# One order string for every iteration of a two-layer attention kernel, in place of eight that repeat

## The chip, the cores and the metric

The kernel runs on one core of one Trainium2 chip. The metric is the device time of the program in microseconds (us). Before the change three runs took 1636.75, 1638.75 and 1639.05 us; the median is 1638.75 us.

## The reference, cut to what matters

The input `x` is 4 x 1024 x 256, the context `ctx_1024` is 4 x 154 x 256. A transformer block (self attention with 16 heads, cross attention to the context, a gated feed-forward) is followed by a second, single-head attention to the same context:

```
x = attention(ln32(x, ln1_s, ln1_b), ln32(x, ln1_s, ln1_b), Wq1, Wkv1, Wo1, bo1) + x
x = attention(ln32(x, ln2_s, ln2_b), context, Wq2, Wkv2, Wo2, bo2) + x
x = geglu_ff(ln32(x, ln3_s, ln3_b), Wff1, bff1, Wff2, bff2) + x
...
attn = softmax((x @ Wq.T + bq) @ (ctx @ Wk.T + bk).T)
x = attn @ (ctx @ Wv.T + bv) + x
```

Self attention over 1024 keys is the largest part. Its softmax subtracts the row maximum, so the scores are computed twice: once to find the maximum, once for the exponential.

## The kernel before, in words

The 4096 rows of `x` are cut into 16 chunks of 256 rows (`NCH`), four to a batch element. A chunk passes through five stages. In `pre` it is normalised and projected to q, k and v, which go to DRAM. In the attention stage it has four units of four heads. `mid` is the output projection, the residual, the second normalisation and q of the cross attention. `cross` is the cross attention. `last` is its output projection, the feed-forward and the second layer.

The stages of different chunks run beside each other. Iteration n (4 to 21) has `pre` of chunk n, attention mostly of chunk n-5 (a little earlier for its maxima), `mid` of chunk n-6, `cross` of chunk n-7 and `last` of chunk n-8. The chunks 0 to 3 have their `pre` in a head before the loop. Iteration 21 (`END`) has what is left: `mid` of chunk 15, `cross` of 14 and 15, `last` of 13, 14 and 15.

What sets the order of work is a string of letters for each iteration. Every engine (SyncE, called SP, issues nearly all DMAs) walks the same string with the function `walk`. At each letter it does its own share of that step, if it has one, and it takes its instructions strictly in that order. Engines are tied to each other by semaphores alone, so SP or ScalarE may be far ahead of TensorE in the string until a wait holds it. The letters are:

- `M`: one 128x512 tile of scores for the maximum (TensorE, line 1679, into one of two PSUM banks) and its reduction (VectorE, line 1360). The matmul of one M waits for the reduction of the M before the last.
- `S`: two score matmuls (line 1697, one of two banks) and one exponential (ScalarE, line 1143). `V`: 16 passes of probabilities times values (line 1709). `Q`, `T`: the maximum of a unit is finished, transposed and stored as two extra rows of q. `O`, `o`: the unit's output is copied (line 1149) and stored (line 801). `u`: q and k of a later unit are loaded.
- `p`, `m`, `c`, `l`: the next step of the chains `pre` (8 steps), `mid` (9), `cross` (36) and `last` (26). In iteration 21 `g` is `cross` of chunk 15, and `k` and `j` are `last` of chunks 14 and 15.
- `x`: q (four DMAs) for `cross` of the next chunk is loaded; for the first chunk of a batch element k and v as well (nine DMAs, lines 714 to 732). `d`: the softmax sums of a cross-attention chunk are loaded (line 672). `i`: VectorE inverts them (line 1244) and SP stores the inverses (line 676). `e`, `f`: the outputs and the inverses are loaded for `last`.
- `s`: a step of the preparation of weights and context.

Steps of `last`, counted from 0, that the text below names: 2 multiplies outputs and inverses (VectorE, line 1249), 3 is the output projection (TensorE, line 1494), 4 the residual and the statistics (VectorE, lines 1255 and 1221), 5 the normalisation, 6 the transposition, 7 to 14 the first feed-forward product (line 1622) with the gate on ScalarE and VectorE, 15 to 18 the second product (line 1631), 19 to 25 the second layer. Step 1 of `mid` inverts the sums of self attention. Steps 1 to 12 of `cross` are its maxima, 13 finishes them, 16 to 35 are scores and values.

There are eight strings: one each for iterations 4 to 7, `STEADY` for 8 to 15, `LATE` for 16 to 19, `FINAL` for 20 and `ENDING` for 21.

Of the kernel before, what the change touches and what calls it, by code (L numbers as in the profile page):

```python
# [21 lines left out]
NCH = B * S // CH  # L22
# [5 lines left out]
NU = NCH * HG  # L28
# [32 lines left out]

FIRST = (
    "sspsssssppsMsMpMMsMsMMpMssMMMMMsMMMpQTMMsMMMMpMpMMsMMsMMs"
)

SECOND = (
    "MMSpSMSQSTSSMMSVSMSMVSMSMSMSMSspSMSVSMMpSsMMSSVMOSpMSSMQVSSTVSMM"
    "sMSSMpMMSSuVSMoSMpSMMVSMoMOpMSMSMSMQusTSSVSMSMSMSMVSMoSMspMMSsMM"  # L70
    "sSSMMVOSMSMVMMQsSSTsSMMSVMSMSMSSMMVMMSSMSMSMSMSMVuMSsMSQVTuO"
)

THIRD = (
    "SSsMMSSMoSMVMSMSSMMVMSMSMuSMSMSMSMSMVpQSmTSVpMOSSMMpSVMSMmSpMSMV"
    "MsSSMpMMSSMpMMSSmVSMuMQpToSVmMOpSoMSMSMSMSMSMSmSsMVMSSVsmMMSSMSo"
    "MSMmSMSMVSQsTmMMVMsOSMSMSMSMVMSMSMSMSSmMMSSMVMusMQxSS"
)

FOURTH = (  # L80
    "sVTSSMMVMsSMSMSOcMuSMScMcuSSMcVMScMSVcSMcSMSopMcSMSSMcSQcVSTScVS"
    "pMSMccOSMSpVSMSMcScpScMSVMSMmpMMcmSMSMcpMcMVMSmSoMcpuQcSTVcmcMSM"
    "pcSMSMcMSMcSMmSOMcSMVcmSMSoMcVSMSMcSMmMcSMQSVuTScSMScMSOVcSMMScm"
    "MMcMdSSMVmMSMSMVMSMSMSeSMixMSSQoVfTVO"
)

STEADY = (
    "uoMSMlcSmpMSMMSSMMSlMMSMcSSMMcVlMMSScclcMuMSScVQSSlccTSSlVScSMcS"
    "MlSmOScMVcMSplMSSpVScMSlpVcMMSlcSMScMpMSlMcSoSVMlMScSpcMMQlTmcpc"
    "MMSclcSVSMpMcSOSMlcMMuSSVVcSSMcMSlocumMMocmSlMmSSMlMlMcMlVQcmTSc"  # L90
    "OVMSmMMclmMSSMcMlSMSMcSMSMVlSMSdMlSMSMVMMQxiSSleTSSVfVlO"
)

LATE = (
    "lMScMMSMSMSuMSlMMSMccSMSMVlcMScMSlMcMSMSQlVcoScSTSVScSlMMSScclSM"
    "VcMcSlOMccSMSSclSmMSVMlSMcMmVScSSMMlcMSSMclMVMSmQcuSlSTcSScVmcSu"
    "oOmMSMclSmSMVcVMSlSmMMclSMcMSmSScMoMlMScMlMMlcSlMMVcmQTlcMVuMSMS"
    "cMlcMOSMScMxSMSVlSMSMMSSMlSMSMdVeMMSSQlSTVViofOl"
)

FINAL = (
    "MMlScSMSMMlSSMMSMMMScMScMVSlMSccMuSlcSMSMcSQVoSlcTclSmVSMMSccSlM"
    "SVccmSMSlMcSSOcMlSVSMMlcMcSSVMSScMMlcMMScSlSVSMcMQSlmcVcSScOmcSm"
    "SVSmSclSScTSmlSSVocoSmclmclclSllSVcSlcSSVcOSclScSlSxVSSSlSSdeVSi"
    "SlSlfOVVo"
)

ENDING = (
    "ccccccccclccocccmcllclcccccccmcmlmclcmlcmccclmlmlkclclcmlcgclxlc"
    "dllllilgggklgeglggggglggkfgglgkkgggglggjggggklkgjggggkggggkgkkkd"  # L110
    "ikkekjkjkkfjkjkjkjjjjjjjjkjjjjjkkjjkkjjjj"
)


def order_of(n):

    if n < LAST_LAG:
        return (FIRST, SECOND, THIRD, FOURTH)[n - MAX_LAG]
    return STEADY if n < NCH else LATE if n < END - 1 else FINAL if n < END else ENDING


CT_STEPS = 3
# [19 lines left out]
def last_set(o):  # L142

    return int(o == NCH - 2)
# [17 lines left out]
def xattn_kernel(nc, t, out):  # L162

    ctx = ExitStack()
    with ctx:
# [340 lines left out]
        def _(sp):  # L506
# [171 lines left out]
            def load_sums(dst, rows, done):  # L678
                for k in range(KD):
                    sp.dma_start(dst[:, k, :], rows.rearrange("(k h w) s -> k h w s", k=KD, w=W)[k, :, 0:DH, :]  # L680
                                 ).then_inc(done, 16)
# [146 lines left out]
        def _(pool):  # L828
# [98 lines left out]
            def last(o):  # L927
                e = last_set(o)
                if e == 0:
                    pool.wait_ge(c_outst, min(o, NCH - 2) * 16)  # L930
                add_bias(xbs[e], x1[1 - (o + LAST_LAG) % 2], bo2, c_xb[1])
                for _ in range(4):
                    yield
                rstd(mv[1], ve[1], rs[1], c_mv[1], c_ve[1], c_rs[1], o + 1)
                yield
                pool.wait_ge(c_x[1], o + 1)
                add_bias(xbs[e], x2s[e], bff2, c_xb[2])
                for _ in range(LAST_STEPS - 5):
                    yield
# [816 lines left out]
```

## Time and profile before

| | |
|---|---|
| median of three runs | 1638.75 us |
| span of the profiled execution, first to last instruction | 1641.9 us |
| TensorE busy (matmul) | 1557.9 us, 95%, 12833 instructions |
| VectorE busy | 1103.1 us, 67% |
| ScalarE busy | 995.2 us, 61% |
| GpSimd busy | 252.9 us, 15% |
| DMA | 129.76 MB, 79 GB/s |
| mean granted TensorE clock | 0.983 |

The profile is of one execution. Its time outside the profiler isn't shown by itself; what is known of it is its span, 3.15 us over the median of the runs. Matmuls are pipelined and the profile models their ends, so TensorE can be "busy" without a pause and still be slower than it could: what counts is the time from the start of one matmul to the start of the next.

### The profile page before, as it was taken

What the parts mean: (1) busy time and instruction counts of PE and PEld (TensorE: products, weight loads), DVE (VectorE), ACT (ScalarE), POOL (GpSimd) and SP (SyncE); (2) the same over time, 40 slices, a digit from 0 to 9 for tenths busy, and PEclk for the clock granted to TensorE, in tenths of its full rate; (3) what the DMA queues carried; (4) which work ended last, traced back from release to release, by engine and by line L of the source; (5) the groups of instructions that cost most, each with busy time, mean ns of one, the idle gap of its engine ahead of it and who ended that gap; (6) DMA issues with size and microseconds to landing.
All of it is one profiled execution on the core that took longest, in us unless ns stands there. A gap on an engine that the chain in (4) does not pass through costs nothing.

```text
span 1641.9 us, 33969 instructions
## 1 busy us (share of the span) xinstructions
PE 1557.9 (95%) x12833; PEld 1011.8 (62%) x12833; DVE 1103.1 (67%) x2269; ACT 995.2 (61%) x2024; POOL 252.9 (15%) x342
## 2 busy tenths in 40 slices
PE   6899999999999999999999999999999999998887
PEld 5454545675757666675767667565656656574766
DVE  4667776858676776858677686858677675843433
ACT  4365667666667566666657566666656555664342
POOL 1210412111112021111112021010011010101110
PEclk9999999999999999999999999999999989997999
DMA  9914242555231412645131321356121311303210
GB/s 236 206 39 139 69 71 83 103 108 109 63 84 46 82 51 72 113 98 119 58 86 47 70 58 58 80 98 116 44 73 35 71 42 44 82 31 73 56 34 13
DMA packets 177116, 129.76 MB, mean 79 GB/s; under 512 B 40975, under 2 KB 168889, under 8 KB 176697
## 3 DMA queue, kind: packets, MB, share of 16 engines
q1 hardware_dynamic: 176889, 127.58, 33.0%
q8 instruction: 101, 1.65, 0.4%
q14 instruction: 62, 0.51, 0.1%
q10 hardware_dynamic: 64, 0.02, 0.0%
HBM read 79.24 MB, written 47.71 MB: 77 GB/s over the span
## 4 chain that ended last, share of the span: by engine, by line
PE 71%; DVE 14%; DMA 7%; ACT 3%; SPq 2%; issue 2%; POOL 0%; DVEq 0%; ACTq 0%; POOLq 0%
PE ps_o L1709 11%; PE ps_max L1679 10%; PE ps_last L1622 10%; PE ps_s L1697 9%; PE ps_last L1631 6%; DVE mxh L1360 6%; PE ps_pre L1486 4%; PE ps_cross L1590 4%; DVE mx L1286 3%; PE ps_pre L1494 3%; PE ps_cross L1576 3%; DMA o_s<-den_c 2%; DMA den<-o_s 2%; PE ps_last L1644 1%; PE ps_last L1659 1%
## 5 line engine op out<-in xcount | busy, mean ns | idle before, releaser
L1360 DVE TENSOR_REDUCE mxh<-ps_max 128x1 f32<-128x512 f32 x1024 | 655.8, 683 | 175.2 <-PE ps_max L1679 173.3
L1143 ACT ACTIVATE probs<-ps_s 128x512 f32<-128x512 f32 x1024 | 579.4, 597 | 232.2 <-PE ps_s L1697 185.4
L1679 PE MATMUL ps_max<-kst,qst 96*128 96x512 bf16 x1024 | 371.5, 386 | 22.0 <-DVE mxh L1360 14.7
L1697 PE MATMUL ps_s<-qst,kst 98*128 98x256 bf16 x2048 | 368.2, 275 | 6.1 <-ACT probs L1143 4.3
L1697 PEld LDWEIGHTS ps_s<-qst,kst 98*128 98x128 bf16 x2048 | 178.8, 98 | 146.6 <-ACT probs L1143 49.4
L1709 PE MATMUL ps_o<-probs,vg 128*17 128x256 f32 x4096 | 268.4, 384 | 0.0
L1679 PEld LDWEIGHTS ps_max<-kst,qst 96*128 96x128 bf16 x1024 | 96.0, 97 | 146.5 <-DVE mxh L1360 91.2
L1087 ACT ACTIVATE probs<-ps_cross 77x512 f32<-77x512 f32 x224 | 132.7, 592 | 78.1 <-PE ps_cross L1576 77.2
L1318 DVE SCALAR_TENSOR_TENSOR th<-th,gb 128x256 f32<-128x256 f32 x128 | 56.9, 445 | 164.3 <-ACT gb L1118 164.3
L1709 PEld LDWEIGHTS ps_o<-probs,vg 128*17 128x17 f32 x4096 | 96.5, 97 | 110.4 <-issue 49.8
L1622 PE MATMUL ps_last<-y_hi,wff_hi 128*128 128x256 f32 x448 | 139.6, 312 | 4.8 <-DVE y_lo L1312 2.5
L1622 PE MATMUL ps_last<-y_lo,wff_hi 128*128 128x256 f32 x448 | 126.9, 283 | 0.0
L1622 PE MATMUL ps_last<-y_hi,wff_lo 128*128 128x256 f32 x448 | 126.6, 283 | 0.0
L1631 PE MATMUL ps_last<-wff,hT 128*128 128x256 f32 x480 | 113.1, 380 | 1.9 <-DVE hT L1321 1.9
L1116 ACT ACTIVATE th<-ps_last,b_tanh 128x256 f32<-128x256 f32 x112 | 53.0, 473 | 89.7 <-PE ps_last L1622 89.7
L1631 PEld LDWEIGHTS ps_last<-wff,hT 128*128 128x128 f32 x480 | 88.9, 190 | 17.2 <-DVE hT L1321 4.3
L885 POOL TENSOR_TENSOR qk_f<-qk_f,qk_parts 128x512 f32<-128x512 f32 x40 | 46.4, 1160 | 323.1 <-ACT qk_f L1076 172.7
L1622 PEld LDWEIGHTS ps_last<-y_hi,wff_hi 128*128 128x128 f32 x448 | 85.3, 190 | 16.0 <-DVE hT L1321 8.4
L1576 PE MATMUL ps_cross<-q2st,k2st 98*77 98x256 bf16 x448 | 86.3, 274 | 2.5 <-ACT probs L1087 2.5
L1622 PEld LDWEIGHTS ps_last<-y_lo,wff_hi 128*128 128x128 f32 x448 | 85.7, 191 | 0.6
L1622 PEld LDWEIGHTS ps_last<-y_hi,wff_lo 128*128 128x128 f32 x448 | 85.6, 191 | 0.0
L876 POOL TENSOR_SCALAR ve<-mv 128x2 f32<-128x2 f32 x34 | 7.7, 226 | 442.7 <-DVE mv L1224 442.7
(261 smaller groups left out, 1951.7 us busy)
## 6 DMA issues: line engine op xcount, KB each, us to landing
parts_s<-qk_parts SPq DMA_DIRECT2D x28, 384.0 KB, 4.3
o_s<-o_sb SPq DMA_DIRECT2D x64, 128.0 KB, 2.6
o_s<-o_sb SPq DMA_DIRECT2D x32, 256.0 KB, 2.2
oT<-o_s SPq DMA_DIRECT2D x62, 128.0 KB
den<-o_s SPq DMA_DIRECT2D x62, 128.0 KB
q_s<-qk_parts SPq DMA_DIRECT2D x16, 384.0 KB, 2.3
q2st<-q_s SPq DMA_DIRECT2D x16, 384.0 KB, 5.3
q2st<-q_s SPq DMA_DIRECT2D x48, 128.0 KB, 6.1
```

The source lines that it names most:

```text
L1087: nc.scalar.activation(probs2[:, h % PR2, :], cross_banks[spare][h % 2][0:CT, :], ACT.Exp, scale=SCALE).then_inc(c_e, 1)
L1143: nc.scalar.activation(probs[:, step % PR, 2 * pair:2 * pair + 2, :].rearrange("p j q -> p (j q)"), ps_s[pair][:, :], ACT.Exp, scale=SCALE ...
L1318: nc.vector.scalar_tensor_tensor(th[:, m % 2, :], th[:, m % 2, :], 1.0, gb[:, m % 2, :], ALU.add, ALU.mult).then_inc(c_gt, 1)
L1360: nc.vector.tensor_reduce(mxh[:, i % PAIRS, i // PAIRS:i // PAIRS + 1], ps_max[i % 2][:, :], AX_X, ALU.max).then_inc(g_mx, 1)
L1486: last = mm(bank[:, m * CH:(m + 1) * CH], w[:, k, m * P:(m + 1) * P], y[:, k, :], start=(k == 0), stop=(k == KD - 1))
L1576: last = mm(cross_banks[spare][h % 2][0:CT, a * CH:(a + 1) * CH], k2st[:, at, a * CT:(a + 1) * CT], q2st[:, at, :], start=True, stop=True)
L1590: last = mm(ps_cross[j * W:j * W + VW, 0:CH], v2[:, a, i * VW:(i + 1) * VW], probs2[:, i % PR2, a * CH:(a + 1) * CH], start=(a == 0), stop ...
L1622: last = mm(last_banks(o)[m % 2][:, part * CH:(part + 1) * CH], wff1[w][:, k, cols_], y3[y][:, k, :], start=(i == 0), stop=(i == len(terms ...
L1631: last = mm(bank_[:, i * D:(i + 1) * D], hTs[e][:, m, i * P:(i + 1) * P], wff2[:, m, :], start=(m == 0), stop=(m == FM - 1))
L1679: mm(ps_max[i % 2][:, :], qst[0:ROWS, h, q * P:(q + 1) * P], kst[0:ROWS, h, half * 512:(half + 1) * 512], start=True, stop=True).then_inc( ...
L1697: last = mm(ps_s[pair][:, j * CH:(j + 1) * CH], kst[:, h, kt * P:(kt + 1) * P], qst[:, h, :], start=True, stop=True)
L1709: last = mm(ps_o[j * W:j * W + VW, 0:CH], vg[:, g, kt, j * VW:(j + 1) * VW], probs[:, step % PR, j, :], start=(kt == 0), stop=(kt == KT - ...
```

## The change

The tuple `ORDERS` holds 18 strings, one for each iteration, and `order_of` picks by iteration. Each letter occurs as often in all 18 as before (3969 letters), and the chains still begin and end in the same iterations, but the shared letters (S, M, V, T, Q, O, o, u, x, d, i, e, f, s) cross the boundaries between iterations: iteration 8 has 70 S and 72 M where it had 64 of each, iteration 9 has 62 and 62, iteration 16 has 59 and 58. Three waits are added, all for chunk 14 alone: the loads of its outputs and inverses, and GpSimd's first addition for it, wait until the last attention unit is copied, because they write into the room of the attention's values.

The diff, with four of the new strings:

```diff
-LATE = (
-    "lMScMMSMSMSuMSlMMSMccSMSMVlcMScMSlMcMSMSQlVcoScSTSVScSlMMSScclSM"
-    "VcMcSlOMccSMSSclSmMSVMlSMcMmVScSSMMlcMSSMclMVMSmQcuSlSTcSScVmcSu"
-    "oOmMSMclSmSMVcVMSlSmMMclSMcMSmSScMoMlMScMlMMlcSlMMVcmQTlcMVuMSMS"
-    "cMlcMOSMScMxSMSVlSMSMMSSMlSMSMdVeMMSSQlSTVViofOl"
-)
...
-ENDING = (
-    "ccccccccclccocccmcllclcccccccmcmlmclcmlcmccclmlmlkclclcmlcgclxlc"
-    "dllllilgggklgeglggggglggkfgglgkkgggglggjggggklkgjggggkggggkgkkkd"
-    "ikkekjkjkkfjkjkjkjjjjjjjjkjjjjjkkjjkkjjjj"
-)
...
+ORDERS = (
...
+    "cclclSMVMSSoMlccSMMSllSScMMSVVuMScSQcSTcSSlMSccMlVccmmSSMMlScMMSSOlMMSSccVlSmuScMMVScSMMlMMcoSSc"
+    "lMMVSSQclTSScVSScOmucMMSScmlMmcuVVcMMSSmMlSSMMcmSSMMlMcMlMcMlSSMMQllmTcSSVcMlScOMMVSSMMclcSSMMcM"
+    "MlSSMVMSMxlSSoMMVdMMQlTlSoSViMSSM",
...
+    "SSVSMMVMMoOSSMSMSMMSMllcccSMMeVlSSccMMSlMSMSMSulQccfSVVSTSccSSlMMSScclVMMOcSSoclMMcSSSlMMccVSSlm"
+    "SScMMVmuSSMcMlcSSMMclScSMMVQlSScVScmmTOumSSlMSSmcVVcMMmcSSMlMMSScmmMMoolMMclcSSMMlcMMllMMocVcQSS"
+    "TlcSMMVcSSMMclSSMMcMOSSMlVMMSSMSMxlMSSMVMMdQulSlSTiVMSMS",
+    "fllMSMSMSeoMccuSSMMVMSMOScMSMVlccMSMMllSccMSSMVmcQSScVTlSSccSMMSlcSSVcMMOSlVcccMMSlMMSScSlMcMmSVS"
+    "SlSSMMcVSScMlMcMSSVcSMcSScmmmmOScQSolcSSVVmSlSSTcVcoSSlcmScSllcllclSlcSSmVcOlcSScxlSSdVSSlSSVSSl"
+    "SSeVOlVi",
+    "coolcccccccccccckfmmclllccccccccclcmmcclmglmccclmclmmcllccllxccllclldggieflgglglgggggglggkkllgkk"
+    "gggggglgggggkkggglggkjjggggkgdkkikkkkkjjkkjjjlkkjjjjkjjjejkjjjjkkjjjkjjfjkj",
 )
...
 def order_of(n):
 
-    if n < LAST_LAG:
-        return (FIRST, SECOND, THIRD, FOURTH)[n - MAX_LAG]
-    return STEADY if n < NCH else LATE if n < END - 1 else FINAL if n < END else ENDING
+    return ORDERS[n - MAX_LAG]
...
                 if o != NCH - 2:
                     sp.wait_ge(c_s3, min(o, NCH - 2))
+                else:
+                    sp.wait_ge(g_o, NU)
                 load_sums(oT2s[last_set(o)], o2_rows(o), c_o2)
...
                 if o != NCH - 2:
                     sp.wait_ge(c_s3, min(o, NCH - 2))
+                else:
+                    sp.wait_ge(g_o, NU)
                 sp.wait_ge(c_inv[1], (o + 1) * 16)
...
                 if e == 0:
                     pool.wait_ge(c_outst, min(o, NCH - 2) * 16)
+                else:
+                    pool.wait_ge(g_o, NU)
```

The new strings shown are those of iterations 16, 19, 20 and 21.

## Rows read from the trace of the kernel before

**Rows 1.** The page: busy time of each engine, and the clock by slices.
```profile
PE 1557.9 (95%) x12833; PEld 1011.8 (62%) x12833; DVE 1103.1 (67%) x2269; ACT 995.2 (61%) x2024; POOL 252.9 (15%) x342
PEclk9999999999999999999999999999999989997999
```

**Rows 2.** Stretches, one iteration each: length, busy PE, PEld, DVE, ACT, POOL, clock, DMA, GB/s.
```profile
148.40:210.13 61.73, 57.75 (x462) 29.25 (x460) 48.68 (x89) 43.15 (x81) 18.33 (x21) 1.00 0.32 103
210.13:288.83 78.70, 74.80 (x666) 39.85 (x665) 56.14 (x111) 52.88 (x104) 17.11 (x20) 0.96 0.34 77
288.83:382.36 93.53, 91.85 (x797) 61.64 (x794) 67.47 (x140) 60.76 (x124) 14.73 (x19) 1.00 0.53 106
568.10:662.86 94.76, 92.16 (x797) 61.38 (x794) 67.42 (x140) 60.71 (x124) 16.14 (x21) 1.00 0.28 69
1036.63:1128.64 92.01, 88.79 (x770) 55.89 (x766) 66.13 (x134) 57.52 (x117) 9.20 (x13) 1.00 0.50 94
1220.52:1312.04 91.52, 88.66 (x770) 55.96 (x766) 65.82 (x133) 57.52 (x117) 9.53 (x13) 1.00 0.24 56
1312.04:1408.90 96.86, 92.36 (x769) 57.67 (x765) 67.03 (x135) 57.63 (x117) 9.20 (x13) 0.95 0.22 56
1408.90:1494.14 85.24, 81.01 (x735) 52.32 (x732) 43.19 (x93) 57.31 (x117) 9.46 (x13) 1.00 0.20 50
1494.14:1641.90 147.76, 120.29 (x774) 93.22 (x770) 60.58 (x144) 52.81 (x120) 17.52 (x25) 0.89 0.15 41
```

**Rows 3.** Chain of waits, 868 to 924: start us, length us, what.
```profile
872.94 0.99 PE ps_o L1709 x16
891.25 0.43 PE ps_max L1679 x2
891.68 1.43 PE ps_last L1622 x12
913.01 1.73 PE ps_last L1631 x8
```

**Rows 4.** Timeline of iteration 17's start: start us, length us, engine, what.
```profile
1129.07 5.47 DVE L1360 TENSOR_REDUCE mxh<-ps_max 128x1 f32<-128x512 f32 x9 [0.29 <-PE ps_max L1679]
1130.41 0.39 PE L1679 MATMUL ps_max<-kst,qst 96*128 96x512 bf16 x1
1130.64 0.39 PE L1697 MATMUL ps_s<-qst,kst 98*128 98x256 bf16 x2
1131.01 0.39 PE L1679 MATMUL ps_max<-kst,qst 96*128 96x512 bf16 x1
```

**Rows 5.** Groups on VectorE, iterations 8 to 19: count, busy us, mean ns, idle before.
```profile
L1360 DVE TENSOR_REDUCE mxh<-ps_max 128x1 f32<-128x512 f32 x768 | 493.0, 683 | 130.6 <-PE ps_max L1679 129.2
L1255 DVE TENSOR_TENSOR x<-ps_last,xb 128x512 f32<-128x512 f32 x24 | 16.4, 684 | 2.6 <-PE ps_last L1631 2.6
```

**Rows 6.** Timeline around 1301 to 1315, SP's issues and VectorE.
```profile
1301.00 0.38 SPq L752 DMA_DIRECT2D o_s<-o_sb  x1
1307.16 0.60 SPq L672 DMA_DIRECT2D den_c<-o_s  x1
1314.03 0.35 DVE L1244 RECIPROCAL den_c<-den_c 128x32 f32<-128x32 f32 x1 [2.62 <-DMA den_c<-o_s]
1314.99 0.61 PE L1679 MATMUL ps_max<-kst,qst 96*128 96x512 bf16 x1 [2.12 <-DVE mxh L1360]
```

**Rows 7.** TensorE in the stretch after that wait.
```profile
1315.00:1325.00 10.00, 10.00 (x48) 0.50 0.32 100
```

**Rows 8.** Timeline of the start of iteration 21.
```profile
1494.19 0.35 DVE L1244 RECIPROCAL den_c<-den_c 128x32 f32<-128x32 f32 x1 [7.81 <-DMA den_c<-o_s]
1503.62 3.78 PE L1494 MATMUL ps_last<-wo,oT 128*128 128x256 f32 x8 [1.28 <-DVE oT L1249]
1505.08 0.35 DVE L1244 RECIPROCAL den_c<-den_c 128x32 f32<-128x32 f32 x1 [1.52 <-DMA den_c<-o_s]
```

**Rows 9.** Chain of waits near the end.
```profile
1586.53 3.30 DMA o_s<-den_c
```

More of the change, by code:

```diff
@@ L59 @@
 PRE_STEPS, MID_STEPS, CROSS_STEPS, LAST_STEPS = 8, 9, 36, 26
-FIRST = (
-    "sspsssssppsMsMpMMsMsMMpMssMMMMMsMMMpQTMMsMMMMpMpMMsMMsMMs"
-)
[L68 to L71, printed above, removed]
-)
[L74 to L92, printed above, removed]
@@ L94 @@
-LATE = (
-    "lMScMMSMSMSuMSlMMSMccSMSMVlcMScMSlMcMSMSQlVcoScSTSVScSlMMSScclSM"
-    "VcMcSlOMccSMSSclSmMSVMlSMcMmVScSSMMlcMSSMclMVMSmQcuSlSTcSScVmcSu"
-    "oOmMSMclSmSMVcVMSlSmMMclSMcMSmSScMoMlMScMlMMlcSlMMVcmQTlcMVuMSMS"
-    "cMlcMOSMScMxSMSVlSMSMMSSMlSMSMdVeMMSSQlSTVViofOl"
[L99 to L106, printed above, removed]
```

39 lines of the change are left out of this document (added).

## The prediction

> **What bounds the kernel now.** I read the page first, then the stretches of one iteration each, then the chain of waits and the timeline where a stretch was longer than its neighbours. The page has TensorE busy for 95% of the span and VectorE for 67% [rows 1]. That looks like a full TensorE, but matmuls overlap in the profile, so I price the steps by the distance from start to start. In the chain 16 passes of V take 0.99 us, two M 0.43, the 12 passes of one feed-forward tile 1.43, and eight passes of a projection 1.73 [rows 3]; an S takes as much as an M, 0.22 (1130.41 to 1130.64, one M's distance to the S behind it) [rows 4].
>
> A full iteration of the middle has 64 M and 64 S (28.2 us), 16 V (15.8), 8 feed-forward tiles (11.4), eleven groups of eight passes (three in `pre`, two in `mid`, six in `last`: 19.0), four groups of cross values at 0.99 and 16 cross scores at 0.22 (7.5), and about 6 us of small tiles. That is 88 us. Iterations 8 to 15 take 1036.63 - 288.83 = 747.8 us, or 93.5 each [rows 2]. So TensorE stands or runs below its price for 44 us there. Iterations 16 to 19 have no `pre` and need 82.4 each, but take 372.3 together [rows 2]: 43 us over. Iteration 20, with 32 M fewer, needs 75.4 and takes 85.2: 10 over. Iteration 6 needs 51 of 61.7, iteration 7 needs 65.5 of 78.7, and iteration 21 needs 98 of 147.8 [rows 2]: 11, 13 and 50 over. Iterations 4 and 5, whose gaps are mostly the preparation of weights, have some 7 us more. A new order can only work on these 178 us; the work itself is the same, letter for letter.
>
> What makes the 44 and the 43 is seen where iteration 17 begins: nine reductions stand in a row on VectorE at 5.47 / 9 = 0.61 us each, and every M behind them starts 0.60 us after the one before, although an M and an S need 0.44 together [rows 4]. There are two banks for M, so a surplus of M over other work can't be stored for long. Where such runs end, VectorE waits for TensorE: 129 us over iterations 8 to 19 [rows 5]. The two engines take turns in waiting; VectorE's total load isn't the bound.
>
> **The change part by part.** *The mix of letters in the middle.* I cut all the old strings, laid end to end, into blocks of 20 letters, added up each engine's durations in a block (M 0.61 on VectorE, and so on), and took what the busier of VectorE and ScalarE has over TensorE. I did it from seven starting points and took the mean. The old order has 8.5 us of such surplus in iterations 4 to 7, 45.5 in 8 to 15, 29.1 in 16 to 20. The new one has 8.6, 37.9 and 22.1. For iterations 8 to 15 surplus and measured standing are nearly the same (45.5 and 44), so 7.6 less is worth 7.6 x 44 / 45.5 = 7.3 us. For 16 to 20 the standing is 53 us, of which 5.3 are an episode priced below; 47 / 29.1 = 1.6 times the surplus. There 7.0 less is worth 11.3 us. What speaks for it: runs such as MSMSM are undone there. Triples in which M and S alternate fall from 82 to 38 in iterations 16 to 20; in 8 to 15 they stay (88 and 90), and in 4 to 7 fall from 105 to 73. Bounds: the surplus of M is stored in two banks only, so a block of 20 letters may be too long a measure and nothing come of it (0); or the ratio of 1.6 may hold in the middle too and the loss be larger than the surplus shows (12 + 13 = 25 us). I take the middle, 18.6. Iterations 4 to 7 I take at 0, between +3 and -5.
>
> *Steps of `last` that follow one another.* The residual (step 4) now comes one letter after the projection it waits for (step 3) in 11 of 16 chunks; before, 12 or 8 letters lay between them for chunks 0 to 12. VectorE takes its instructions in order, so it stands for as much of the 1.73 us [rows 3] as its backlog doesn't cover, and behind it stand the reductions on which the next M wait. In the old order VectorE waited 2.6 us before 24 residuals in iterations 8 to 19, and these waits are for line 1631, so at step 19; at step 4 there was none [rows 5]. Usually two or three reductions (0.61 each) are in the backlog, and two M can run ahead; what is left is 0 to 1.9 us a chunk. I take 0.25 for 12 chunks: 3 us lost, with bounds 0 and 23.
>
> *The wait for the softmax sums at letter i.* Iteration 19 is 96.86 - 91.52 = 5.3 us longer than 18, with the same string [rows 2]. There x has nine DMAs to issue, for a new batch element, and stands in front of d: the store of the outputs goes out at 1301.00, the load of the sums at 1307.16, and VectorE waits at i until 1314.03, 2.62 us; TensorE stands 2.12 us [rows 6]. Then its granted clock is 0.50 (1.2 GHz) for 10 us [rows 7]. In the new iteration 19 the x still stands in front of d, and the TensorE work between the last step of cross 11 and its i is 8.4 us in place of 10.8. I expect the same episode with up to 2.4 us more: 2 us lost; bounds -5.3 (it goes) and +5. For the Trainium skill, page "TensorE: Matmul & The Clock Gate", section "Terms", the penalty is the time at the lower clock times the share of clock that is missing; that would be 5 us here plus the wait of 2.1, against 5.3 by rows, since part of the iteration goes at VectorE's pace anyway.
>
> *The added waits.* The last attention unit is copied as iteration 21 begins (1494.14 [rows 2]). SP reaches e and f of chunk 14, and GpSimd the first step of its `last`, after that in string order. Behind SP's wait stand its other DMAs, behind GpSimd's the bias for `mid` 15. All of them come later than the copy anyway: 0 us, at most 1.
>
> *Iteration 21.* Before, f stood between i and o on SP and had to wait for the stored inverses, so the last outputs of attention were stored after it, and `mid` 15 inverted its sums at 1505.08 [rows 8]. The new string has both o in front of f and the inversion in front of step 13 of cross 14: some 3 us earlier. But projection 13 (1503.62) keeps its place behind its own loads, and x of chunk 15 keeps waiting for the last scores of cross 14. The inversion for chunk 15 moves one feed-forward tile forward; behind it lie a store of 3.30 us [rows 9] and a load before projection 15. The 12 maxima of cross 15, a little over half a us each on VectorE and 0.2 on TensorE, are spread over the second feed-forward product of chunk 13. I count 2 us for the first, 1 for the second, 1 for the third: 4 gained, between 0 and 10.
>
> **Sum.** 7.3 + 11.3 - 3 - 2 + 4 = 17.6 us less than the profiled span of 1641.9: 1624.3. The runs shown stand 3.15 us below that span, so the forecast is 1621 us.
>
> **The rivals.** *More waits like that of iteration 19 (slower).* The spacing of c, x, d, i and of steps 3 and 4 now differs in every iteration and is no longer the one that holds eight times over. Wherever VectorE stands at an i or at a step 4 longer than the two banks reach, TensorE stands and its clock halves, at 5.3 us an episode [rows 2, 6, 7]. The gain of 17.6 is gone with three more episodes than counted, and from four on the kernel is slower. With five it takes 1621 + 26.5 = 1648 us. For it: 11 steps 4 are close to their steps 3. Against it: between the last step of a cross and its i lie 5.7 to 8.9 us of TensorE work in iterations 8 to 19, where the old order had 5.5 in `STEADY`, with a clock of 1.00 in those iterations [rows 2]. *Nothing comes of the mix.* If the surplus that counts is that of two banks, the new order merely shifts the standing: 0 from the mix, +3 and +2 from the waits, -4 at the end; 1640 us. For it: the alternating runs of 8 to 15 are as many as before. *All of it comes.* Both parts of the mix at 1.6 (12 and 11), the episode of iteration 19 goes (5), iteration 21 gains 10, nothing is lost behind step 3: 1639 - 38 = 1601 us. For it: iteration 21 has 50 us of standing, the most of all.
>
> **How the numbers follow.** The forecast has 0.58, more episodes 0.13, nothing 0.11, all of it 0.18. Within 0.2% is 1635.5 to 1642.0 us, about what a measurement can tell from no change. The forecast and "all" are faster: 0.76; "nothing" is 0.11, the episodes are 0.13. The likeliest case's own range is 1611 to 1631 us; with half of each outer case left out it is 1602 to 1642.
>
> **What would show it.** VectorE's wait before M (129 us over iterations 8 to 19) should fall by some 15 us, and the time from the start of iteration 16 to the start of 21 from 457.5 us by about 9, with fewer M spaced at 0.60 us. VectorE's waits at line 1255 for line 1494 should grow by a few us, and the clock should be half near 1315, near 220 and near 1500 again. Iteration 21 should last 144 us. It would be wrong if the waits at line 1244 or 1255 grew to over 20 us with more half-clock stretches before iteration 20, or if the middle iterations kept their 93.5 us.

## The result: slower by 0.6%, where 1.1% faster was forecast

| | before | after |
|---|---|---|
| median, seven runs each | 1638.75 us | 1648.92 us |
| lowest to highest | 1636.75 to 1644.52 | 1643.83 to 1662.00 |
| ratio, 95% interval | | 1.0063 [1.0034, 1.0092] |
| profiled execution | | 1662.0 us, span 1660.2 us |
| mean granted TensorE clock in it | 0.983 | 0.973 |

The profiled execution of the new kernel is the slowest of its seven, 13.1 us above their median. That of before spans 1641.9 us. A time is 1.8 us over its span in the profiled executions whose time is known (1662.0 and 1660.2 us here), so this one stood about 5 us above its own median; the 3.15 us ahead of the prediction set a span against a time. So the profiles show 18.3 us more span for a difference of 10.2 us between the medians, and a single number from the new one may be too large by almost a half.

In kernel.py of the new kernel the lines below the order strings have moved, SP's loads and stores by 1 to 5 and what follows the added waits by 7: maxima L1686 and their reduction L1367, the reciprocal at i L1251, step 2 of `last` L1256, step 3 L1501, step 4 L1262; SP's load of the sums L673, store of the inverses L677, their load L686. Busy time is what it was [rows 1], and the clock row has two slices below 9, as before. The page alone doesn't show where 18 us went:

```profile
PE 1558.7 (94%) x12833; PEld 1024.2 (62%) x12833; DVE 1106.5 (67%) x2269; ACT 988.4 (60%) x2024; POOL 250.0 (15%) x342
PEclk9899999999999999999999999999999999998999
```

Stretches of one iteration each, in the columns of [rows 2]: iterations 7, 8, 11, 16, 17, 19, 20 and 21.

```profile
203.70:279.00 75.30, 72.46 (x656) 38.80 (x654) 55.81 (x108) 52.68 (x103) 15.35 (x19) 0.98 0.36 82
279.00:379.90 100.90, 97.92 (x848) 63.87 (x845) 73.73 (x152) 64.38 (x131) 14.70 (x20) 1.00 0.51 105
576.50:670.00 93.50, 90.41 (x778) 61.27 (x776) 65.03 (x136) 57.76 (x120) 15.94 (x21) 0.98 0.25 66
1059.20:1147.30 88.10, 84.55 (x734) 56.31 (x735) 61.84 (x128) 53.23 (x110) 9.16 (x13) 0.98 0.44 88
1147.30:1243.40 96.10, 89.32 (x746) 58.36 (x745) 63.95 (x130) 56.64 (x117) 9.23 (x13) 0.95 0.27 61
1335.60:1437.00 101.40, 92.89 (x794) 59.27 (x792) 68.42 (x141) 58.87 (x121) 10.00 (x15) 0.97 0.29 61
1437.00:1518.60 81.60, 80.05 (x743) 53.00 (x743) 42.99 (x95) 56.27 (x118) 8.09 (x12) 1.00 0.22 55
1518.60:1660.20 141.60, 115.52 (x774) 91.68 (x770) 61.70 (x142) 52.42 (x120) 16.93 (x25) 0.92 0.15 42
```

Lengths alone mislead here, because the new iterations don't hold the same work (8 has 848 matmuls, before 797). So I took each step's start-to-start time less its back-to-back price (0.22 us for an M or an S, 0.99 for a V, 1.73 for a projection, as in [rows 3, 4]) and summed what is over, by iteration. The split "step 3" is what TensorE stands right before `last` step 3 (the output projection) and what this projection takes over its price:

| us over back-to-back | 4-7 | 8-15 | of it step 3 | 16-19 | of it step 3 | 20 | 21 | all |
|---|---|---|---|---|---|---|---|---|
| before | 62.6 | 42.5 | 5.3 | 42.1 | 1.4 | 9.9 | 46.4 | 203.5 |
| after | 58.1 | 67.4 | 21.9 | 50.8 | 17.2 | 5.9 | 40.3 | 222.5 |

All together 19.0 us more, for a span that is 18.3 us longer. The head (4 to 7) gives 4.5, iterations 20 and 21 give 10.1, and 8 to 19 lose 33.6, of which 32.4 stand before or in step 3. That is the surprise, and the waits name it. First the new kernel, TensorE's own waits over iterations 8 to 19 (us in all, times, longest), then the same wait before the change:

```profile
PE ps_last L1501 <- DVE oT L1256: 24.7, 10, 4.8
PE ps_max L1686 <- DVE mxh L1367: 8.4, 14, 3.6
```

```profile
PE ps_last L1494 <- DVE oT L1249: 4.4, 6, 1.7
```

And VectorE's groups over the same stretch, in the columns of [rows 5]:

```profile
L1367 DVE TENSOR_REDUCE mxh<-ps_max 128x1 f32<-128x512 f32 x776 | 496.6, 682 | 116.3 <-PE ps_max L1686 113.7
L1256 DVE TENSOR_TENSOR oT<-oT,den 128x512 f32<-128x512 f32 x24 | 16.5, 686 | 31.0 <-DMA den<-o_s 23.0 <-DMA oT<-o_s 8.0
L1262 DVE TENSOR_TENSOR x<-ps_last,xb 128x512 f32<-128x512 f32 x24 | 16.4, 685 | 9.8 <-PE ps_last L1501 7.6 <-PE ps_last L1638 2.2
```

VectorE waits 15.5 us less before M than in [rows 5], just as forecast (113.7 for 129.2). But it waits 31.0 us at step 2's multiply, 23.0 of them for the load of the inverses (`den`) and 8.0 for the load of the outputs (`oT`, letter e); before the change it waited 4.2 us there, all for `den`. One such place in order of time, chunk 1 in iteration 9 (start us, length us, engine; SPq is an issue of SP):

```profile
374.76 0.54 SPq L673 DMA_DIRECT2D den_c<-o_s  x1
378.21 0.67 SPq L812 DMA_DIRECT2D qst<-sh_hi  x1
378.50 0.35 DVE L1251 RECIPROCAL den_c<-den_c 128x32 f32<-128x32 f32 x1 [0.32 <-DMA den_c<-o_s]
378.92 0.66 SPq L812 DMA_DIRECT2D qst<-sh_lo  x1
379.62 0.58 SPq L677 DMA_DIRECT2D o_s<-den_c  x1
385.28 1.26 SPq L686 DMA_DIRECT2D den<-o_s  x2
392.36 0.69 DVE L1256 TENSOR_TENSOR oT<-oT,den 128x512 f32<-128x512 f32 x1 [4.86 <-DMA den<-o_s]
393.11 3.78 PE L1501 MATMUL ps_last<-wo,oT 128*128 128x256 f32 x8 [4.77 <-DVE oT L1256]
396.93 0.69 DVE L1262 TENSOR_TENSOR x<-ps_last,xb 128x512 f32<-128x512 f32 x1 [1.59 <-PE ps_last L1501]
```

The chain of waits has the two transfers in it. The clock was 1.00 while the store was under way; in the window that begins about 2 us into TensorE's stand it is 0.50, the level of 1.2 GHz:

```profile
379.62 5.59 DMA o_s<-den_c
385.94 6.40 DMA den<-o_s
```

```profile
379.62:385.21 5.59, 5.28 (x39) 2.44 (x31) 5.35 (x10) 3.81 (x8) 1.30 (x2) 1.00 0.77 154
390.30:397.10 6.80, 3.99 (x12) 3.09 (x13) 3.15 (x6) 0.00 (x0) 0.00 (x0) 0.50 0.77 134
```

To be read as: the chain behind the last step of a cross attention is the store of its outputs, d (load of 16 KB of sums), i (invert), a store of 16 KB, f (load of the inverses, two transfers of 128 KB), step 2's multiply, step 3. Nothing in it is long by itself, and every link waits for the one before to land. In chunk 1 the store of the inverses took 5.59 us and their load 6.40. The Trainium skill, page "DMA: Bandwidth & Descriptors", section "Anatomy of one DMA — SWDGE (gpsimd) path", gives a fixed cost of about 2.0 us and bytes over 436e3; by that an estimate is 2.0 us for 16 KB and 2.3 for 128 KB. Its fit is for another way of issuing, and the trace disagrees in this place, though the median of the 16 KB stores, 1.8 us, is near it. The DMA engines were 77% busy in both windows above; that this made the two transfers slow is not shown.

TensorE stood 4.77 us, and the projection then took 3.78 us for 1.73. From the end of the last cross step to step 3 the chain took 19.6 to 21.6 us for chunks 0 to 9 before, and 21.1 to 24.3 us now.

### The profile page after: what moved, and what is told of

The parts are those of the page before. It is cut to its first block, busy times and chain, and to the rows that moved or that the text cites. A ratio compares the mean times of both kernels' runs of the same rounds, so it can differ in the third digit from the quotient of the medians.

```text
span 1660.2 us, 33968 instructions
## 1 busy us (share of the span) xinstructions
PE 1558.7 (94%) x12833; PEld 1024.2 (62%) x12833; DVE 1106.5 (67%) x2269; ACT 988.4 (60%) x2024; POOL 250.0 (15%) x342
## 4 chain that ended last, share of the span: by engine, by line
PE 71%; DMA 10%; DVE 8%; SPq 4%; ACT 4%; issue 3%; POOL 0%; DVEq 0%; POOLq 0%; ACTq 0%
PE ps_max L1686 10%; PE ps_o L1716 10%; PE ps_s L1704 10%; PE ps_last L1629 10%; PE ps_last L1638 6%; PE ps_pre L1493 4%; PE ps_cross L1597 3%; PE ps_pre L1501 3%; PE ps_cross L1583 3%; DMA den<-o_s 3%; DMA o_s<-den_c 3%; DVE mxh L1367 2%; PE ps_last L1501 2%; DMA den_c<-o_s 1%; PE ps_last L1666 1%
## 5 line engine op out<-in xcount | busy, mean ns | idle before, releaser
L1367 DVE TENSOR_REDUCE mxh<-ps_max 128x1 f32<-128x512 f32 x1024 | 654.1, 682 | 158.0 <-PE ps_max L1686 154.6
L1150 ACT ACTIVATE probs<-ps_s 128x512 f32<-128x512 f32 x1024 | 572.3, 597 | 286.0 <-PE ps_s L1704 243.7
L1686 PE MATMUL ps_max<-kst,qst 96*128 96x512 bf16 x1024 | 347.3, 386 | 17.8 <-DVE mxh L1367 10.5
L1704 PE MATMUL ps_s<-qst,kst 98*128 98x256 bf16 x2048 | 354.2, 275 | 4.7 <-ACT probs L1150 2.6
L1704 PEld LDWEIGHTS ps_s<-qst,kst 98*128 98x128 bf16 x2048 | 177.0, 98 | 140.9 <-ACT probs L1150 50.8
L1686 PEld LDWEIGHTS ps_max<-kst,qst 96*128 96x128 bf16 x1024 | 94.7, 98 | 126.2 <-DVE mxh L1367 85.3
L1716 PEld LDWEIGHTS ps_o<-probs,vg 128*17 128x17 f32 x4096 | 98.1, 97 | 114.3 <-issue 46.2
L1325 DVE SCALAR_TENSOR_TENSOR th<-th,gb 128x256 f32<-128x256 f32 x128 | 60.9, 476 | 156.8 <-ACT gb L1125 156.5
L1629 PEld LDWEIGHTS ps_last<-y_hi,wff_hi 128*128 128x128 f32 x448 | 85.4, 191 | 18.3 <-DVE hT L1328 12.2
```

What stands on the lines that cost most here:

```text
L1150: nc.scalar.activation(probs[:, step % PR, 2 * pair:2 * pair + 2, :].rearrange("p j q -> p (j q)"), ps_s[pair][:, :], ACT.Exp, scale=SCALE ...
L1325: nc.vector.scalar_tensor_tensor(th[:, m % 2, :], th[:, m % 2, :], 1.0, gb[:, m % 2, :], ALU.add, ALU.mult).then_inc(c_gt, 1)
L1367: nc.vector.tensor_reduce(mxh[:, i % PAIRS, i // PAIRS:i // PAIRS + 1], ps_max[i % 2][:, :], AX_X, ALU.max).then_inc(g_mx, 1)
L1629: last = mm(last_banks(o)[m % 2][:, part * CH:(part + 1) * CH], wff1[w][:, k, cols_], y3[y][:, k, :], start=(i == 0), stop=(i == len(terms ...
L1686: mm(ps_max[i % 2][:, :], qst[0:ROWS, h, q * P:(q + 1) * P], kst[0:ROWS, h, half * 512:(half + 1) * 512], start=True, stop=True).then_inc( ...
L1704: last = mm(ps_s[pair][:, j * CH:(j + 1) * CH], kst[:, h, kt * P:(kt + 1) * P], qst[:, h, :], start=True, stop=True)
```

## The experiments

Theory A: the new order loses at this chain. Most chunks had 17.4 to 17.6 us of TensorE work between the last cross step and step 3, and still have 17.1 to 17.7; but i stands 7.5 to 8.9 us behind the last cross step in most chunks (5.5 in the old `STEADY`, 10.9 in the old `LATE`), and f, where SP loads the inverses, at 9.2 to 20.9 (9.2), behind other issues. Theory D: the mixture of shared letters is what costs, and step 3 only shows it. Ratios are to the kernel before, run beside each on the same chip. Its median was 1643.06 us beside runs 1 to 4, 1639.13 beside 5 to 8 and 1641.95 beside 9 to 12, so runs of different groups are compared by their ratios, as recorded; these are not quite the quotients of the medians. The strings in the edits are cut to the place that changes. (Theory B, in the first expectations, is the first form of D.) All but the second kernel carry the three added waits; the order strings are written shorter in them, so their lines are 31 below the new kernel's.

**1 and 2. The inverses not waited for.**

```diff
-                sp.wait_ge(c_inv[1], (o + 1) * 16)
-                load_inv(den2s[last_set(o)], o2_rows(o), c_o2)
+                sp.wait_ge(c_inv[0], (o + 1) * 16)
+                load_inv(den2s[last_set(o)], o1_s.rearrange("(o r) s -> o r s", o=NCH)[o], c_o2)
```

These two kernels multiply by the wrong inverses: they leave out a wait that the result needs, and only price it.

In the new kernel: 

> The new order, unchanged, but the loads of the inverse sums for `last` (letter f) read the rows of self attention's inverses of the same chunk, which were stored long before, so they no longer wait for the store of the inverses at letter i. The values are those of the wrong sums; number and size of the DMAs stay. Theory A (the chain of small DMAs from the last step of cross through d, i and f to step 2 of last is what makes TensorE stand before step 3): the stretches before and in step 3 of chunks 0 to 11, over 35 us over their price in the profiled execution, go for the most part; 1615 to 1628 us. Theory B (the loss is from the mix of M, S and the rest, or from residuals that follow their projection by one letter): no more than 5 us faster, 1643 to 1649 us.

In the kernel before: 

> The same edit on the order before. Theory A: the chain has 11.9 us of TensorE work to hide behind there and costs only the longer stretches in iterations 11 and 15 and some in 16 to 21; 1628 to 1638 us. Theory B says the same, since it doesn't look at this chain: this run is the control.

Measured 1631.47 us in the new order (ratio 0.9938 [0.9914, 0.9962]) and 1638.47 in the old (0.9982 [0.9968, 0.9997]). The first is 3.5 us above theory A's range and 11.5 below theory B's; the second is half a us above its range. With this wait gone the new order is the faster one; with it, the slower. Step 3 of chunks 0 to 11 stands 18.4 us (39.2), of which 5.7 are chunk 9, whose e, the load of the outputs, stands behind the letters of steps 2 and 3 themselves. (18.4 in place of 39.2: the inverses explain 21.) Outside step 3, iterations 8 to 15 stay at 45.2 us, where the old order has 37.2: so something in the new strings costs 8 us there, whatever the load of the inverses does.

**3. e right behind d, f right behind i, for chunks 1 to 13.**

```diff
 (end of iteration 9)
-SMMVSMMSlSMSxdMVMMQlSTiSlV
+SMMVSMMSlSMSxdeMVMMQlSTifSlV
```

> The new order with the letters e and f alone moved, for chunks 1 to 13: e directly behind d, f directly behind i (or behind step 21 of the chunk before, where that comes later). Nothing is left out. Theory A: SyncE issues the load of the inverses as soon as they are stored, 2 us after the store in place of 2 to 7.6, and the standing before step 3 shrinks by about half: 1625 to 1637 us. Theory B: no change, 1645 to 1652 us.

Measured 1649.91 us, 1.005 [1.003, 1.007]: a miss for theory A, in theory B's range. Step 3's standing did fall, 39.2 to 13.9 us, and VectorE's wait at step 2's multiply from 31.0 to 11.7, with d and i where they were. But TensorE now stood before the first maxima of `cross`, for k, 7.5 us (2.0 in the new kernel), and once for q before an M, 4.5 us (1.9). Iterations 8 to 19:

```profile
PE ps_last L1470 <- DVE oT L1225: 8.4, 5, 2.3
PE ps_cross L1534 <- DMA k2st<-k_s: 7.5, 3, 2.9
PE ps_max L1655 <- DMA qst<-parts_s: 4.5, 1, 4.5
```

SP takes its letters in order. At an f that comes this early it waits for the store of the inverses to land, and what stands behind it (x, T, u) is issued late. SP's waits for that store at f, over the same iterations, first the new kernel, then this run:

```profile
SPq L787 <- DMA o_s<-den_c: 22.1, 9, 3.9
```

```profile
SPq L756 <- DMA o_s<-den_c: 50.1, 12, 7.4
```

The earliest place isn't the best one.

**4. The old order with the new ending (iteration 21, and 20 ending in SlSlOVV).**

```diff
-    "SlSlfOVVo"
+    "SlSlOVV"
...
-ENDING
+the new string of iteration 21
```

> The order before with the new string for iteration 21 alone (and one o and one f fewer at the end of iteration 20, since the new string has them). In the profiled executions iteration 21 took 138.0 us with the new string and 144.2 with the old. If that is the string's doing: 1632 to 1635 us. If it is what iteration 20 hands over: 1638 to 1641 us.

Measured 1637.85 us, 0.9982 [0.9965, 0.9999]: 3 us faster by the ratio, with an interval that barely excludes no gain at all. The time misses the range of the first reading (1632 to 1635) and is just under that of the second (1638 to 1641); by its ratio it lies between them. Iteration 21 is 40.6 us over, 5.8 less than before, as in the new kernel; but run 5, which keeps the old string there, has 42.0 in its profile, so 5.8 may be too much. The ending gives a little by itself, some 3 us.

**5. The old order, only steps 2 and 3 of `last` 3.1 us earlier, in iterations 8 to 15.**

```diff
-uoMSMlcSmpMSMMSSMMSlMMSMcSSMMcVlMMSScclcMu
+uoMSMlcSmpMSMMSSMMSllMMSMcSlSMMcVMMSScccMu
```

> The old order, with only steps 2 and 3 of `last` (the multiply by the inverses and the output projection) moved 3.1 us of TensorE work towards the front in the eight iterations 8 to 15; step 4 and every other letter stay. Theory A (the cost of the new order is TensorE standing at step 3 because the chain of small DMAs, sums loaded, inverted, stored, loaded again, ends later than step 2 wants it): the old order had 17.4 us of TensorE work between the end of the last cross-attention step and step 3 and did not stand, so its margin is at most about 3 us; with 14.3 us each of eight chunks stands 1.5 to 4 us before step 3 and runs it at half clock (3.5 instead of 1.7 us): 25 to 45 us of standing, of which other waits may give back a half. 1652 to 1680 us, with eight more stretches at half clock. Rival D (the new order loses by its mixture of shared letters, and step 3's standing is only where it shows): this order keeps the old mixture, so within 4 us of the kernel before, 1636 to 1643 us.

Measured 1688.66 us, 1.0307 [1.0278, 1.0336]: theory A, and 9 us beyond its range. The mixture is the old one, and yet it is the worst kernel so far; the margin of the old chain was under 3.1 us in `STEADY`. This run also shows how the stand reaches TensorE. Chunk 0, in order of time:

```profile
293.39 0.39 PE L1655 MATMUL ps_max<-kst,qst 96*128 96x512 bf16 x1 [0.21 <-DVE mxh L1336]
297.16 0.69 DVE L1225 TENSOR_TENSOR oT<-oT,den 128x512 f32<-128x512 f32 x1 [3.82 <-DMA den<-o_s]
297.76 2.08 DVE L1336 TENSOR_REDUCE mxh<-ps_max 128x1 f32<-128x512 f32 x3
298.51 0.61 PE L1655 MATMUL ps_max<-kst,qst 96*128 96x512 bf16 x1 [4.51 <-DVE mxh L1336]
299.72 3.62 PE L1470 MATMUL ps_last<-wo,oT 128*128 128x256 f32 x8
```

VectorE stands 3.82 us at step 2's multiply. Behind it in its own order stand the reductions of the M already made; both banks are full, so the next M waits 4.51 us, three letters before step 3 is even reached. Step 3 itself hardly stands (13.7 us for all), but runs at half clock. Over iterations 8 to 19 TensorE waited for reductions like this (before: 8.5 us, 27 times, longest 2.1):

```profile
PE ps_max L1655 <- DVE mxh L1336: 41.9, 38, 6.6
```

**6. The new order with d, i, e and f of chunks 1 to 12 at the old distances.**

```diff
 (end of iteration 9, start of 10)
-SMMVSMMSlSMSxdMVMMQlSTiSlV   cMMeSSMSMScMSMVMfSMcSo
+SMMVSMMdSlSMSxMVMMiQlSTeSlV   cMMfSSMSMScMSMVMSMcSo
```

> The new order, with the letters d, i, e and f of chunks 1 to 12 put at the distances that the old order's iterations 8 to 15 have, in us of TensorE work behind the last cross-attention step: d 2.5, i 5.5, e 7.6, f 9.2 (the new order has i at 7.5 to 8.9 and f at 9.2 to 20.9 in most chunks). Nothing else moves. Theory A: the inverses leave 2 to 3 us earlier and the loads are no longer issued behind stores and other loads, so the standing before and in step 3 for chunks 0 to 11 falls from 39.2 to under 15 us, and, unlike with e and f right behind d and i, SP does not hold the loads of the next chunk's q back: 1625 to 1638 us. Rival D (mixture): 1645 to 1650 us, whatever step 3 does. Rival E (the queue gives back what it is relieved of, as with e and f right behind): step 3 falls and the standing turns up at other waits, 1642 to 1650 us.

Measured 1639.05 us, 0.9995 [0.9973, 1.0016], one us above the range of theory A, below those of D and E, and all of the change's loss is back. Only the place of four letters in twelve chunks differs from the new kernel. Over iterations 8 to 19:

```profile
PE ps_last L1470 <- DVE oT L1225: 7.9, 5, 2.4
PE ps_max L1655 <- DMA qst<-parts_s: 4.5, 1, 4.5
```

Step 3's standing is 10.7 us for chunks 0 to 11 (39.2; before 6.8), 18 stretches at half clock became 12 (before 8). Outside step 3 iterations 8 to 15 keep their 45.3. VectorE's wait at the multiply is 10.9 us, hardly less than run 3's 11.7. So theory A holds for what made the new order slower than the old. Why the middle is still no gain without that is not told by this run: theory D's mixture is one reading, the new places of the steps another. The profiled execution of this run is 3.5 us below its median and that of the new kernel 13.1 above, so the profiles are 26.5 us apart where the ratios are 0.0068, or 11 us.

**7 and 8. Steps 2 to 14 of `last` later; and both edits together.**

```diff
 (iteration 9)
-MMVlScuScMMSllccSSVSMMcQSScVTSSlmccMSMSlcSS
+MMVScuScMMSccSSlVSMMcQlSSclVTSSmccMSMScSSl
```

> The new order, with steps 2 to 6 of `last` of chunks 0 to 10 moved 2.3 to 2.6 us of TensorE work towards the end (step 4 by 3.9, so that it no longer stands next to step 3), steps 7 to 14 by ever less (2.6 down to 0.4), and steps 2 to 6 of chunk 11 by 1.0 to 2.6; no DMA letter moves. Theory A: 2.4 us more for the chain takes most of the standing before step 3: from 39.2 to under 15 us for chunks 0 to 11, and the wait of the residual (7.6 us behind the projection) to under 3; 1625 to 1640 us. Rival D (mixture): 1645 to 1650 us.

> The new order with both edits, the letters d, i, e, f at the old distances and steps 2 to 14 of `last` later. Theory A: the standing before step 3 is gone (under 8 us for chunks 0 to 11, as in the kernel before), and what is left is the new order's saving: 1618 to 1632 us, below the kernel before. Rival D (mixture): 1643 to 1650 us. Rival E (given back elsewhere): 1636 to 1645 us.

Measured 1746.61 us, 1.066 [1.0632, 1.0689], and 1762.84 us, 1.0758 [1.0731, 1.0785]. Both expectations are far off, and neither theory foresaw it. What they said of step 3 came: 8.0 and 6.1 us of standing for chunks 0 to 11. But iterations 8 to 15 were 126 us over, spread over many small stands. VectorE's waits over 330 to 1210 us, first the new kernel, then run 7:

```profile
DVE th L1325 <- ACT gb L1125: 90.0, 64, 2.5
DVE y_lo L1319 <- ACT y_hi L1117: 4.0, 9, 0.7
```

```profile
DVE th L1294 <- ACT gb L1094: 137.3, 65, 5.1
DVE mxh L1336 <- PE ps_max L1655: 97.7, 117, 3.4
```

In each step of the first feed-forward product VectorE needs ScalarE's part of the gate. VectorE stands there 2.1 us at a time in place of 1.4, and in its own order the reductions behind it wait. By the strings the moved step comes behind more exponentials in ScalarE's order; that this is the whole of it was argued and not shown.

**12. Only steps 2 to 6 later.** This one asks what in run 7 it was.

```diff
 (iteration 9)
-MMVlScuScMMSllccSSVSMMcQSScVTSSlmccMSMSlcSS
+MMVScuScMMSccSSlVSMMlcQlSScVTSSmccMSMSlcSSl
```

> The new order with only steps 2 to 6 of `last` of chunks 0 to 11 later (2 and 3 by 2.1 us of TensorE work, 4 by 2.2, 5 by 1.3, 6 by 0.5); the steps of the first feed-forward product stay where they are, and no DMA letter moves. It tells apart why moving steps 2 to 14 cost 100 us although the standing before step 3 fell to 8.0 us: there VectorE waited 137 us for ScalarE's part of the gate in the window 330:1210, against 90 us in the new order. Theory F (each step of the feed-forward product must stand where ScalarE's gate is not queued behind exponentials when VectorE comes to it): with these steps unmoved the 100 us are not there; step 3's standing falls to 10 to 15 us, and steps 5 and 6, now closer (0.2 to 0.9 us), give a part back: 1632 to 1645 us. Rival G (moving steps 2 to 6 past their neighbours is what cost it): 1680 to 1745 us.

Measured 1671.58 us, 1.02 [1.0164, 1.0236]: between the two, outside both ranges. Between it and run 7 lie 75 us: the moved feed-forward steps (F), whose wait is back at 93.2 us, and a somewhat larger move of steps 5 and 6. What is left is a loss of 23 us against the new kernel. In the same stretch VectorE has one more wait for ScalarE, 23.5 us for the copy behind step 6 (4.0 in the new kernel). TensorE stands at step 6 itself, the transposition, for step 5's normalisation (`oT`, L1204), and at step 7 for what follows that copy (`y_lo`):

```profile
DVE y_lo L1288 <- ACT y_hi L1086: 23.5, 9, 3.5
PE ps_last L1454 <- DVE oT L1204: 13.8, 8, 5.3
PE ps_last L1598 <- DVE y_lo L1288: 7.8, 4, 2.6
```

In the new kernel the wait at the transposition isn't there and that at step 7 is 0.2 us. So steps 5 and 6 that follow one another closely are a part of what is left; how the loss splits between the two waits stays open.

**11. The old distances, and step 4 apart from step 3.**

```diff
 (iteration 9)
-VlScuScMMSllccSSVSMM
+VlScuScMMSlccSSlVSMM
```

> The new order with d, i, e, f at the old distances, and step 4 of `last` of chunks 0 to 11 moved 0.5 to 1.3 us of TensorE work behind step 3, next to which it stands in the new order. The trace of the new kernel has 7.6 us of VectorE waiting there for the projection, 6 times, in iterations 8 to 19. If TensorE loses that time at the maxima behind it: 4 to 8 us less than with the old distances alone (1639), 1631 to 1635 us, and iterations 8 to 15 fall from 45.3 to about 40 us over (without step 3). Rival (the wait hides in the reserve before M): 1637 to 1641 us.

Measured 1645.17 us, 1.0025 [1.0002, 1.0049]: no gain, rather a loss, above both ranges (run 6, measured on another chip: 0.9995 [0.9973, 1.0016]; the intervals overlap). Iterations 8 to 15 went to 53.4 us over outside step 3, from 45.3. So no run shows that the 7.6 us of VectorE waiting at step 4 cost anything, and the place next to step 3 is not a fault.

**9 and 10. What the parts are worth when they are kept apart.** Run 9 has the new iterations 4 to 7, the old 8 to 20, the new 21. Run 10 has in addition the new 16 to 20 with the old distances of d, i, e, f.

```diff
 (run 9: end of iteration 7, then STEADY as before)
-...SSMcmMMVdSSMMVS
+...SSMcmMMVdSSMMVSMMSMSMSeSMixMSSQoVfTVO
```

> The new strings for iterations 4 to 7, the old ones for 8 to 20, the new one for 21 (the shared letters that the new head leaves over, 22 of them, stand at the end of iteration 7; iteration 20 ends in SlSlOVV). Above back-to-back work the new head has measured 4.5 to 9.7 us less than the old one (62.6 against 58.1, 55.0, 57.1, 54.1 and 54.8), the new iteration 21 5.8 us less (46.4 against 40.6). If these parts add up and nothing is given back at the joints: 1638.7 - 6 - 4 = 1627 to 1633 us, with iterations 8 to 20 as before (94.5 us over). Rival (the head's gain is work pushed to iteration 8, which must pay it): 1634 to 1639 us.

> The new head as in the run before, the old string in iterations 8 to 15, and the new strings from 16 on with d, i, e and f at the old distances (13 shared letters, the difference of the two counts, stand at the end of iteration 15). Without step 3's standing, the new iterations 16 to 19 have measured 31.0 and 33.6 us above back-to-back work where the old ones have 40.7, and 39.4 in the run with the old distances, of which 4.6 is one wait behind an i in iteration 19. So, if the mixture of LATE is a real gain of the change and that of STEADY is not: 4 to 9 us below the run with the new head alone, 1620 to 1631 us. Rival (LATE gives nothing once its chain is mended): level with the run with the new head alone, 1630 to 1638 us.

Measured 1630.21 us, 0.9928 [0.9905, 0.9952], and 1628.42 us, 0.9909 [0.9881, 0.9937]. Both are in the ranges of their first readings, though run 10 is 1.8 us below run 9 where 4 to 9 were expected, and both beat both kernels. Run 9 gains 0.0072, 12 us, of which run 4 gives the ending some 3; the head wasn't run alone. Whether the new 16 to 20 are worth anything once mended can't be told from the times, as the intervals overlap, nor from the profiles: they have 191.1 and 181.1 us over, but that of run 10 is 8.5 us below its own median. Iterations 16 to 19 have 40.7 and 40.1. A wait of 4.5 us for q is left there, at an M of iteration 19:

```profile
1389.75 5.18 DMA qst<-parts_s
1394.98 0.61 PE ps_max L1655
```

The last of the four loads of q (letter u) goes out at 1389.75, behind the store of the inverses at 1387.52, since i stands in front of u there. The new kernel, with i behind u and T, stands 1.92 us at that M.

The profiles in one table, us over back-to-back work; "8-15 rest" is without step 3:

| kernel | 4-7 | 8-15 rest | 16-19 rest | step 3, 8-19 | 20, 21 | span of the profile | median us | ratio |
|---|---|---|---|---|---|---|---|---|
| before | 62.6 | 37.2 | 40.7 | 6.7 | 56.3 | 1641.9 | 1638.75 | 1 |
| after | 58.1 | 45.5 | 33.6 | 39.1 | 46.2 | 1660.2 | 1648.92 | 1.0063 |
| 1, free inverses | 55.0 | 45.2 | 31.0 | 18.3 | 45.8 | 1633.1 | 1631.47 | 0.9938 |
| 6, old distances | 54.8 | 45.3 | 39.4 | 10.5 | 44.7 | 1633.7 | 1639.05 | 0.9995 |
| 9, new head, old middle | 57.9 | 38.5 | 39.2 | 5.4 | 50.1 | 1628.0 | 1630.21 | 0.9928 |
| 10, new ends, old `STEADY` | 53.1 | 39.0 | 38.4 | 6.2 | 44.4 | 1618.1 | 1628.42 | 0.9909 |

## Why the prediction was wrong, step by step

*The step that failed* is the one the sum doesn't have: the cost at step 2's multiply, behind the chain of d, i, the store, e and f, was put at nothing without a reason. The prediction asked of each chunk whether VectorE would stand at i or at step 4, and how much TensorE work lies "between the last step of a cross and its i". It took the 5.7 to 8.9 us there for more room, a point against the rival. That looks at the wrong place: its own sign, waits of over 20 us at the line of i or of step 4, didn't come (5.4 and 16.9 us, before 3.0 and 11.5), while VectorE waited 31.0 us at the multiply, before 4.2. It cost 32.4 us in the profiled execution for iterations 8 to 19. By the runs the new order gains 0.0125 by not waiting for the inverses, some 20 us, and the old one 0.0018, 3 us (1 and 2).

Which letter of the chain did it is known in part. In `STEADY` what is left for the store and the load before step 2 fell from 10.7 us (i to step 2) to 6.5 to 8.2 in most chunks. But the old `LATE` has only 5.6 us there in three of its chunks and VectorE stands 0.3 us at most at their multiplies; chunks 3 and 4 keep 10.7 and 10.5 in the new order and lose 3.3 and 4.0 us at step 3; and run 3, with d and i left where the new order has them, takes VectorE's wait from 31.0 to 11.7 us. So most of it hangs on where e and f stand among SP's other issues, and less on i. In `LATE` f went from 10.8 us behind the last cross step to 11.4, 12.5, 16.8 and 20.9, e from 5.9 to as much as 18.9. Run 6 moved all four letters, so what d and i give by themselves stays open.

*The mix, 18.6 us.* For 8 to 15, -7.3 was forecast and +8.3 measured outside step 3. These iterations took 97.5 us each (279.00 to 1059.20; their 25 more M and S are 0.7 of it), where 93.5 was already to be a sign of being wrong. Iterations 16 to 20 took 459.4 us, where 457.5 was to fall by 9. The mechanism is in the trace as foretold, and yet doesn't pay: VectorE's wait before M fell 15.5 us, and M that follow M stand 4.1 us in all, before 9.2. I split the standing of iterations 8 to 15 outside step 3 by its size: stands of under 0.6 us fell from 36.2 to 33.7 us in all, those above it rose from 0.9 to 11.8 (9.9 in run 6), at cross maxima, at M and before feed-forward steps. A measure that adds up engine work in blocks of 20 letters sees the first kind and not the second, a single latency that isn't met; the old `STEADY`, eight times over, had nearly none. What made the new ones is not shown. For 16 to 20, -11.3 was forecast, and 33.6 + 5.9 against 40.7 + 9.9 is -11.1 in the new kernel, of which some 3 are the episode of iteration 19 below. With the wait for the inverses gone it holds (31.0 + 7.7, run 1), with the chain mended it is 39.4 + 7.2, or -4.0 (run 6). So the forecast's size came where the letters of the chain stand as in the new kernel; mended, half or less is left in these profiles.

*Iterations 4 to 7*, taken at 0 with +3 to -5: -4.5, and -4.7 to -9.7 in the experiments' profiles. This was undersized; no experiment tells which part of the head it is.

*Step 4 next to step 3, +3:* by the strings the residual comes one letter after its projection in 9 of 16 chunks, not 11. VectorE waited 7.6 us for the projection, and run 11 shows that parting them gains nothing. The term was 0 as far as the runs show. *The wait at i in iteration 19, +2:* VectorE stands 1.07 us at this i (1434.92), TensorE 1.92 us at an M just behind, for q, and the clock is 1.00 over 1432 to 1440, where [rows 7] have 0.50. The episode went, which is -3.4 us by the old price of 5.3 less the 1.92. *The added waits, 0:* no wait of SP, GpSimd or TensorE for them shows.

*Iteration 21, -4:* 147.76 to 141.60 by the stretches, so -6.2; run 4, with this string alone, gives some 3 us, near the term. The stands at its start are 1.09, 2.93 and 1.59 us where [rows 8] have 7.81, 1.28 and 1.52:

```profile
1518.48 0.35 DVE L1251 RECIPROCAL den_c<-den_c 128x32 f32<-128x32 f32 x1 [1.09 <-DMA den_c<-o_s]
1527.24 0.35 DVE L1251 RECIPROCAL den_c<-den_c 128x32 f32<-128x32 f32 x1 [1.59 <-DMA den_c<-o_s]
1529.04 3.78 PE L1501 MATMUL ps_last<-wo,oT 128*128 128x256 f32 x8 [2.93 <-DVE oT L1256]
```

*The rival* of more episodes had the right shape: VectorE stands at a letter of the DMA chain, TensorE stands and its clock halves. Five episodes were to give 1648 us, and 1648.92 came, but that is luck. Its place was wrong (step 2's multiply, not i or step 4), and so was the number: nine of twelve chunks lose 2 to 7 us each at step 3, and the stretches at half clock are 18 (90.6 us) in place of 8 (59.3 us), 9 of them in iterations 8 to 19, where there was 1. That it was given 0.13 is the second fault: the argument against it was read from the wrong distance.

## What to carry to other kernels

When an order is laid out anew, price the chains of latency before the mixture of work: for every value that goes out by DMA and comes back, add up the measured time of its links and hold it against the work that lies between its first and last letter, link by link, since a letter moved later in the middle of the chain takes from all behind it. Look at what stands in the same queue in front of each link, and remember that issuing a waiting DMA earlier only moves the stand to what is queued behind it (run 3). Keep the parts of a new layout that measure better, here its two ends, and leave a tuned steady state alone until an experiment says otherwise (runs 9, 10).

## What the runs showed that I had not expected

- The cost of a stand grows on its way: in run 5 VectorE waited 26.8 us at the multiply over iterations 8 to 19 (before 4.2), TensorE 41.9 us for the reductions behind it (before 8.5), and the kernel lost 49.5 us; projections behind such stands took up to 3.8 us for 1.73.
- A DMA of 16 KB landed after 1.8 us in the median, but after 5.59 us in chunk 1, in a stretch with the DMA engines 77% busy (first window above).
- Moving 13 small steps of one chain by at most 3.9 us of TensorE work, with nothing added, cost 98 us beyond the new kernel (run 7); the wait that grew most by name is VectorE's for ScalarE at the gate, 90.0 to 137.3 us.
